# Turning the first step's state back in four events, its split on GpSimd

## The reference, cut to what matters

```python
q = _l2norm(q)
k = _l2norm(k)
state = q
for _ in range(STEPS):          # STEPS = 2, BETA = 1
    sim = jnp.einsum('bqhd,bkhd->bqhk', state, k)
    att = jax.nn.softmax(BETA * sim, axis=-1)
    state = jnp.einsum('bqhk,bkhd->bqhd', att, v)
o = state.reshape(B, S, H) @ Wo + bo
```

## Time and profile before

| what | value |
|---|---|
| median of 3 runs | 3548.38 us (3545.81 to 3549.18) |
| the profiled execution | 3555.46 us |
| its span, first to last instruction | 3553.7 us |
| mean granted TensorE clock | 0.961 |
| PE busy | 3247.1 us, 19974 matmuls |
| DVE busy | 2401.4 us, 5281 instructions |
| ACT busy | 2082.6 us, 2689 instructions |
| POOL busy | 1219.1 us, 2291 instructions |
| costliest group | ACT exponentials (L810), 1574.6 us, 1536 of 1025 ns |
| next | DVE maxima (L1041), 1249.6 us, 1024 of 1220 ns |

### The profile page before, as it was taken

One profiled execution on the slowest core, in us unless ns is written; L12 is line 12 of the kernel. 1 busy time (PEld: TensorE's weight loads), 2 busy tenths in 40 slices (PEclk: granted clock), 3 DMA queues, 4 the chain that ended last, 5 costly groups with the idle time before them and its releaser, 6 DMA issues.

```text
span 3553.7 us, 55360 instructions
## 1 busy us (share of the span) xinstructions
PE 3247.1 (91%) x19974; PEld 1682.0 (47%) x19974; DVE 2401.4 (68%) x5281; ACT 2082.6 (59%) x2689; POOL 1219.1 (34%) x2291
## 2 busy tenths in 40 slices
PE   5888998989999899999999999999999999998999
PEld 2444444444444444454444445444444444444567
DVE  2636675847678676767767676776867677775662
ACT  2454666656666666666666666566666656564442
POOL 3314242342424334242522424252342425222321
PEclk8989999989999999999999999999999999998999
DMA  1000000001110100111001011110001111000110
GB/s 41 4 28 5 31 4 29 31 4 34 31 34 28 31 9 30 34 32 34 29 31 34 5 34 31 34 31 28 34 4 34 31 34 32 30 29 4 59 33 34
DMA packets 81502, 96.89 MB, mean 27 GB/s; under 512 B 50544, under 2 KB 68400, under 8 KB 81104
## 3 DMA queue, kind: packets, MB, share of 16 engines
q1 hardware_dynamic: 81232, 93.35, 8.2%
HBM read 82.76 MB, written 4.78 MB: 25 GB/s over the span
## 4 chain that ended last, share of the span: by engine, by line
PE 53%; DVE 15%; ACT 14%; POOL 10%; issue 7%; SPq 1%; DMA 0%; ACTq 0%; DVEq 0%; POOLq 0%
PE ps L679 14%; PE ps L696 13%; ACT probs L810 12%; PE ps L751 7%; DVE negmax L1041 6%; PE ps L761 5%; PE ps L579 5%; PE ps L716 3%; PE ps L585 2%; PE ps L574 2%; DVE uts L1007 1%; POOL qT L1235 1%; POOL xe L1258 1%; POOL qk L1199 1%; DVE stats L907 1%
## 5 line engine op out<-in xcount | busy, mean ns | idle before, releaser
L810 ACT ACTIVATE probs<-ps 128x1024 f32<-128x1024 f32 x1536 | 1574.6, 1025 | 1070.6 <-PE ps L679 1056.2
L1041 DVE TENSOR_REDUCE negmax<-ps 128x2 f32<-128x1024 f32 x1024 | 1249.6, 1220 | 468.4 <-PE ps L716 451.9
L679 PE MATMUL ps<-qT,kT 32*128 32x512 f32 x3072 | 786.5, 507 | 109.8 <-ACT probs L810 57.4
L696 PE MATMUL ps<-probs,v 128*32 128x512 f32 x6144 | 851.8, 627 | 0.0
L1258 POOL TENSOR_TENSOR xe<-xT_m,G 128x512 f32<-128x512 f32 x288 | 367.2, 1278 | 1045.3 <-PE ps L751 997.2
L751 PE MATMUL ps<-xe,w_sb 128*128 128x256 f32 x2304 | 668.2, 416 | 7.9 <-DVE hid L1100 4.1
L679 PEld LDWEIGHTS ps<-qT,kT 32*128 32x128 f32 x3072 | 291.9, 185 | 763.8 <-ACT probs L810 493.7
L716 PE MATMUL ps<-kT,qT 32*128 32x512 f32 x2048 | 529.4, 512 | 93.7 <-DVE negmax L1041 90.1
L751 PEld LDWEIGHTS ps<-xe,w_sb 128*128 128x128 f32 x2304 | 406.8, 196 | 185.3 <-issue 136.9
L1098 DVE SCALAR_TENSOR_TENSOR th<-th,ps 128x256 f32<-128x256 f32 x576 | 236.8, 411 | 216.6 <-ACT th L840 214.2
L840 ACT ACTIVATE th<-ps 128x256 f32<-128x256 f32 x576 | 221.7, 385 | 180.4 <-PE ps L751 170.1
(11 more groups left out here) (169 smaller groups left out, 2652.8 us busy)
## 6 DMA issues: line engine op xcount, KB each, us to landing
G<-gates_dram SPq DMA_DIRECT2D x96, 768.0 KB, 6.2
maxrow<-negmaxT SPq DMA_DIRECT2D x512, 2.0 KB
v<-v_tok SPq DMA_DIRECT2D x256, 18.0 KB, 1.9
X<-in_x SPq DMA_DIRECT2D x16, 256.0 KB, 2.9
out<-X SPq DMA_DIRECT2D x16, 256.0 KB, 2.3
w_sb<-in_w SPq DMA_DIRECT2D x1, 1152.0 KB, 7.0
w_sb<-in_w SPq DMA_DIRECT2D x1, 576.0 KB, 8.7
gates_dram<-gT SPq DMA_DIRECT2D x32, 18.0 KB
```

The lines of the kernel that those rows point to most:

```text
L679: nc.tensor.matmul(ps[:, B_ST + h, :], kT[a][rows, g * S + kc * P:g * S + (kc + 1) * P], qT[a][rows, g * S:(g + 1) * S], start=True, stop= ...
L696: ins = nc.tensor.matmul(ps[ROWS * j:ROWS * (j + 1), B_UT, :], v[:, at:at + ROWS], probs[:, n % QUADS, j, :], start=(kc == 0), stop=(kc == ...
L810: nc.scalar.activation(probs[:, quad % QUADS, j:j + 2, :], ps[:, B_ST:B_ST + 2, :], ACT.Exp).then_inc(sem["exp_done"], 1)
L1041: nc.vector.tensor_reduce(negative[:, tc, 2 * half:2 * half + 2], ps[:, B_SM:B_SM + 2, :], AX_X, ALU.max, negate=True).then_inc(sem["sm_re ...
```

## The change

VectorE's `uts_state` ends with the first transpose. A new event, `divide`, is placed at w + 11.2: VectorE (lag 0) takes the reciprocal and multiplies there; GpSimd (lag 1.0, so w + 12.2) waits for it and makes both parts of `qstack`. `state` moves from w + 11.2 to w + 13.4: VectorE waits for GpSimd's split and transposes, and GpSimd casts at w + 14.0. Two semaphores, `state_divided` and `state_split`, are added.

```diff
--- before.py
+++ after.py
@@ -47,6 +47,7 @@
 SM_AT = (0, 1, 2, 3, 5, 6, 8, 9)
 JOB = 10
 PV_AT = 3.6
+DIVIDE_AT, STATE_AT = 11.2, 13.4
 S1_AT = (0, 8, 16, 40)
 S2_AT = (48, 64, 80, 88)
 S2_MAX_AT = (31, 42, 63, 73)
@@ -97,7 +98,7 @@
     "dve": {**{n: HOP for n in "sm ffn_y p0_qkv p1_qkv turn o_y m_logits m_down m_probs fold".split()},
             "m_gu": 2.0, "turn": 1.4, "p1_qkv": 1.0, "sm": 0.6, "uts": 0.4, "p0_qkv": 1.0, "ffn_y": 1.0},
     "pool": {**{n: HOP for n in "ffn_stats p0_stats p1_stats m_stats p0_sums p0_hi p1_hi m_index state".split()},
-             "rows": 2 * HOP},
+             "rows": 2 * HOP, "divide": 1.0},
     "sp": {"m_gt": 2 * HOP, "p1_values": HOP},
     "pe": {},
 }
@@ -221,7 +222,8 @@
         t.at(start + 2 * kc + PV_AT, "pv", kind, b, g, kc)
     t.at(start + 10.2, "uts", kind, b, g)
     if kind == "S1":
-        t.at(start + 11.2, "state", b, g)
+        t.at(start + DIVIDE_AT, "divide", b, g)
+        t.at(start + STATE_AT, "state", b, g)
     else:
         t.at(start + 11.2, "turn", kind, b, g)
 
@@ -429,7 +431,7 @@
         gates_in = [ctx.enter_context(nc.semaphore(f"gates_in{i}")) for i in range(3)]
         sem = signals(nc, ctx, "dve_step pool_step "
                                "st_ready exp_done pv_done ut_copied sm_ready sm_read mx_ready "
-                               "state_turned state_done rows_in rows_added o0_part o1_part o_added "
+                               "state_divided state_split state_turned state_done rows_in rows_added o0_part o1_part o_added "
                                "ffn_var ffn_r ffn_biased ffn_done "
                                "p0_var p0_r p0_res p0_squared p0_summed p0_unit p0_hi p0_lo "
                                "p1_var p1_r p1_res p1_hi p1_lo v_moved "
@@ -1006,17 +1008,16 @@
                 dve.wait_ge(sem["pv_done"], TC * (n + 1))
                 nc.vector.transpose(uts[:],
                                     ps[:, B_UT, :]).then_inc(sem["ut_copied"], 1)
-                dve.wait_ge(sem["ut_copied"], n + 1)
+
+            def divide(n, b, g):
+                dve.wait_ge(sem["ut_copied"], window_no("S1", b, g) + 1)
                 link(nc.vector.reciprocal(rden[:], s1t[:, :, HD]))
-                link(nc.vector.tensor_tensor(st8[:], s1t[:, :, 0:HD],
-                                             rden[:].unsqueeze(2).to_broadcast([P, TC * NG, HD]), ALU.mult))
+                nc.vector.tensor_tensor(st8[:], s1t[:, :, 0:HD], rden[:].unsqueeze(2).to_broadcast([P, TC * NG, HD]),
+                                        ALU.mult).then_inc(sem["state_divided"], 1)
 
             def state(n, b, g):
 
-                twice = qstack[:, :, 0:2 * HD].rearrange("p x (r d) -> p x r d", r=2).bitcast(F32R)
-                link(nc.vector.tensor_copy(twice, st8[:].unsqueeze(2).to_broadcast([P, TC * NG, 2, HD])))
-                link(nc.vector.tensor_tensor(qstack[:, :, 2 * HD:3 * HD].bitcast(F32R), st8[:], qstack[:, :, 0:HD],
-                                             ALU.subtract))
+                dve.wait_ge(sem["state_split"], n + 1)
                 nc.vector.transpose(uts[:],
                                     qstack[:].rearrange("p x e -> p (x e)")).then_inc(sem["state_turned"], 1)
 
@@ -1109,7 +1110,7 @@
                                         ALU.add).then_inc(read_signal(key), 1)
 
             play("dve", dict(fold=fold, masks=masks, ffn_stats=ffn_stats, ffn_y=ffn_y, p0_stats=p0_stats, p0_qkv=p0_qkv, p0_sums=p0_sums, p0_hi=p0_hi,
-                      p1_stats=p1_stats, p1_qkv=p1_qkv, p1_hi=p1_hi, turn=turn, uts=uts_state, state=state, sm=sm, mx=mx_turn, o_y=o_y,
+                      p1_stats=p1_stats, p1_qkv=p1_qkv, p1_hi=p1_hi, turn=turn, uts=uts_state, divide=divide, state=state, sm=sm, mx=mx_turn, o_y=o_y,
                       m_stats=m_stats, m_logits=m_logits, m_probs=m_probs, m_index=m_index, m_gu=m_gu, m_down=m_down))
 
         @block.gpsimd
@@ -1224,6 +1225,14 @@
                 pool.wait_ge(sem["p1_hi"], n + 1)
                 low_parts(heads1(i), qk_heads(1, i), i, sem["p1_lo"])
 
+            def divide(n, b, g):
+
+                pool.wait_ge(sem["state_divided"], n + 1)
+                twice = qstack[:, :, 0:2 * HD].rearrange("p x (r d) -> p x r d", r=2).bitcast(F32R)
+                link(nc.gpsimd.tensor_copy(twice, st8[:].unsqueeze(2).to_broadcast([P, TC * NG, 2, HD])))
+                nc.gpsimd.tensor_tensor(qstack[:, :, 2 * HD:3 * HD].bitcast(F32R), st8[:], qstack[:, :, 0:HD],
+                                        ALU.subtract).then_inc(sem["state_split"], 1)
+
             def state(n, b, g):
                 pool.wait_ge(sem["state_turned"], n + 1)
                 nc.gpsimd.tensor_copy(qT[0][:, g * S:(g + 1) * S],
@@ -1259,7 +1268,7 @@
                                         ALU.mult).then_inc(sem["m_xe"], 1)
 
             play("pool", dict(ffn_stats=ffn_stats, ffn_bias=ffn_bias, p0_stats=p0_stats, p0_res=p0_res, p0_squares=p0_squares,
-                      p0_sums=p0_sums, p0_hi=p0_hi, p1_stats=p1_stats, p1_res=p1_res, p1_hi=p1_hi, state=state, rows=rows,
+                      p0_sums=p0_sums, p0_hi=p0_hi, p1_stats=p1_stats, p1_res=p1_res, p1_hi=p1_hi, divide=divide, state=state, rows=rows,
                       m_stats=m_stats, m_index=m_index, m_xe=m_xe))
 
 
```

## The result

The changed kernel takes 3461.8 us in the median of 4 runs (3456.9 to 3464.9) against 3548.8 us for the kernel before: 87 us or 2.5% less, ratio 0.9753 (95% interval 0.9741 to 0.9765). The direction was forecast; the size was not: the forecast was 3498 us, and the range ended at 3465. The profiled execution took 3461.28 us, with a span of 3459.5 us and a mean granted clock of 0.982 (before 0.961).

A forecast was written before the change was run, and what follows sets the result against it. TensorE was taken as the bound, through stalls on VectorE's `negmax`. Stalls of 30 us plus clock of 21 us gave 51 us off, 3497 us for the median, stated as 3498 us, with a range of 3465 to 3542.

The forecast's parts named there:

- The bound: TensorE, busy 91%, bounds the run; its longest waits are for VectorE's `negmax`, 90.1 us in 120 waits.
- The stall term: PE's waits at the four state events shrink by 2.05 us a turn net, 30 us in all.
- The first event: VectorE's transpose alone, without reciprocal and multiply, lets the reduction start earlier: 2.1 us a turn saved.
- The fourth window: Multiply replaces copy, subtract, transpose before a 0.85 us PE wait: 0.7 us saved, at least 0.4 if GpSimd holds it.
- The third event: State's transpose, two slots later ahead of another reduction, costs 0.75 us a turn, 0.5 of it in the first window.
- The clock term: Shorter PE waits spare falls of TensorE's clock: 0.01 in a regular turn's mean clock, 21 us.
- The upper bound of 42 us: Most the clock term could give: 0.02 of clock in each of 14 regular turns.
- GpSimd's part: Copy 0.4 us and subtract 0.45 us, 64 times, 61 us with the link, costed at nothing beside other work.
- The new wait: VectorE's wait for GpSimd's split before the second transpose: margins of 1.5 us or more, costed at nothing.
- Stalls alone: Rival: the waits shrink but the clock falls as before; 30 us gained, 3518 us, chance 0.23.
- taken back: Rival: PE's gain is lost to waits elsewhere in the turn; 0 to 10 us gained, 3543 us, chance 0.10.
- slower by the wait for the split: Rival: VectorE's third event waits for GpSimd, delaying the reduction and PE; 3559 to 3621 us, taken as 3590, chance 0.11.

The follow-up runs named there:

- Experiment 5: Kernel before, with 26 expert half units ahead of the first and second windows' stalled score pairs issued twice: 3509.3 us, ratio 0.9888.
- Experiment 10: Changed kernel with GpSimd's split at 12.0 slots instead of 12.2, ahead of `m_index`: 3460.6 us, ratio 0.9741.
- experiment 9: Changed kernel with the second transpose at 12.4 slots instead of 13.4: 3480.8 us, ratio 0.9806.
- experiment 3: Kernel before with copy, subtract and second transpose at 13.4 slots instead of 11.2, all on VectorE: 3571.3 us, ratio 1.0057.
- Experiment 4: Kernel before with reciprocal and multiply moved from behind the first transpose to the head of the second event at 11.2 slots: 3528.2 us, ratio 0.9926.
- experiment 1: Changed kernel without GpSimd's part: copy and subtract on VectorE, with the second transpose at 13.4 slots: 3517.9 us, ratio 0.9909.

## Why the prediction was right or wrong

*The bound, right.* PE's waits for `negmax` at the four state events were the place; they fell by 37 us where 40 were forecast.

*The stall term, right in its sum.* 2.05 us a turn were forecast. Summed over the regular turns, PE's waits at the state events fell from 4.1 to 1.8 us a turn: 2.26 us, 25 us in 11 turns where 22.6 stood. Experiment 5 gives nearly the same from the times. It has the old stalls and the changed kernel the new ones, at a clock that rounds to 1.00 and 0.99: 2220.9 less 2200.3 is 20.6 us, and to that come 5 to 6 us, since the changed kernel has 17 us more low time. The parts came otherwise than forecast, and two errors cancelled. The first event gave 2.4 us a turn and not 2.1, since PE waits 0.53 and 0.44 us where it had waited 1.30 and 1.20. The fourth window gave 0.33 of 0.85 us and not 0.7. By the text's own figures its lower bound was 1.0 less 0.43, 0.57 us, and not the 0.4 that it names; the measured value lies below both, because the score pair ahead came 0.74 us earlier, and not 0.43, and so took more of that 1.0. The multiply was held by GpSimd, as the row of the held copy had warned and as the Trainium skill (GPSIMD Engine Reference, Specifications) has it for instructions with two SBUF inputs. The trace agrees: 1.02 us beside `xe`, 0.29 without. The third event cost PE a wait of 0.35 us in the first window (0.5 was given) and 0.14 in the second (nothing was).

*The clock term, the step that failed.* "I take the middle, 0.01, 21 us." The price in it was near: 1.5 us per 0.01 of a 205 us turn is 0.37 us for each us of low time, and experiment 5 measured 0.32 to 0.36. The number of falls spared was too small. The regular turns went from 0.97 to 0.99, two times the step taken, and their low time from 137 to 34 us: of their 58.7 us some 25 are stalls and 33 the clock, where 22.6 and 16.5 stood. Over the run the low time went from 277 to 125 us, and 152 us at 0.32 to 0.36 are 49 to 55 us, where 21 stood; that leaves 32 to 38 of the 87 us to the stalls and to what is not accounted for. The trace of the kernel before had the answer. Of the 24 falls in its regular turns, 18 begin between 0.3 us before and 2.4 us behind the end of a wait that the change shortens (10 at the second window's, 4 at the first's, 4 at the fourth's 0.85 us), and these hold 96 of the 137 us; 5 of the others begin at the first window's wait of 0.9 us ahead of its state event, which the change leaves. The prediction had two of the 18 in its rows and named them (the one at 1223.1 begins right at the wait's end, most do not), and still went to the middle between nothing and all, as if nothing were as likely. What is left of the clock's cost fits: of the changed kernel's 8 falls, 5 begin 0.3 to 3.0 us behind that same wait of 0.9 us, three of them around the wait of 0.53 us that now follows it. One of the 5 (timeline, then a stretch, PEclk as the last number but two):

```profile
1370.33 0.50 PE L718 MATMUL ps<-kT,qT 32*128 32x512 f32 x2 [0.90 <-DVE negmax L1042]
```

```profile
1370.80:1374.20 3.40, 3.40 (x13) 1.70 (x16) 3.37 (x7) 0.98 (x2) 2.76 (x8) 0.50 0.02 5
```

The upper bound of 42 us was too low as well, for it left out the irregular parts. What lies outside the 11 turns I had summed at 12 us (three turns more at 3.55 and the 1 us for the first blocks); it gave 35.5 us (22.7 and 12.8), at clocks that went from 0.94 to 0.95 and from 0.95 to 0.98. How much of the start's share is stalls I can't tell; the same kernel again had 10 us less of it.

The Trainium skill (TensorE: Matmul & The Clock Gate, HAM oscillation), which ties falls to longer idle gaps than these and by which the sum would have been 30 us, is not enough for this kernel: experiment 5 took away no stall, only the idleness in two waits of 1.3 and 1.2 us a turn, and the low time fell by 115 us. Nor does the length of a wait alone decide. In the same regular turns PE has 22 waits of 1.0 to 1.3 us at L579, and no fall of the clock begins in the 3 us behind any of them (kernel before, timeline, then a stretch):

```profile
1365.95 0.66 PE L579 MATMUL ps<-id_sb,stack0q 128*128 128x128 f32 x4 [1.33 <-POOL stack0q L1207]
```

```profile
1360.00:1400.00 40.00, 36.32 (x240) 18.95 (x237) 16.71 (x27) 30.13 (x44) 12.05 (x12) 1.00 0.05 8
```

What sets the waits at the state events apart from these was not tried.

*GpSimd's part, right.* 0.40 and 0.46 us, foreseen at 0.4 and 0.45; hidden. *The new wait, right in its cost and wrong in its margin:* 2.9 us in 4 cases, but with 0.03 us to spare in the second window and not 1.5. Experiment 10 shows that VectorE would not have been earlier anyway.

*The signs.* Those of the forecast came: `negmax` waits of 52.8 us, no wait at the third window's first event nor at the fourth's, regular turns at 0.99, hardly any wait for the split. None of them could tell 3498 us from 3462: the low time summed over the run could.

*The rivals.* Stalls alone, taken back, and slower by the wait for the split all fell; experiment 9, which moves the transpose towards the split, still has only 7.4 us of that wait. What I left out was a combination: that the parts would not add up. Alone the later place would have made the kernel slower (experiment 3), with no more waiting for `negmax`, by the clock.

*Open:* why a wait at L579 spares the clock and one as long at a state event does not; the share of stalls in the start's 22.7 us; and why experiment 9 runs its last stretch at a lower clock. Experiment 4 gained 23 us where the profiled execution's waits (8 us less) and low time (9 us less, some 3 us) account for 11. That execution has the lowest clock of its four (0.962; the others 0.965 and 0.966). By the medians of all runs on that chip, 0.9655 against 0.962, the low time is 27 us less, some 9 us, and what stays open is within the interval.

## What to carry to other kernels

When an engine's burst stalls TensorE for about a microsecond, count the stall twice: once as it stands, and once for the clock behind it; here the second was the larger. Look at the granted clock in the stretch right behind each wait of PE, and do so for every fall of the regular turns and not for two: count how many begin at the waits you are removing, and how much low time they hold. Take the price from turns at different clocks, and that share of the sum rather than half of it. A cheap test of such a case is to leave the stall and keep PE busy in it.

## What the runs showed of the hardware

TensorE doing 26 half units twice made the kernel 41 us faster, since the granted clock stayed at 1.00 in turns where it had been 0.97. Waits of PE of 0.85 to 1.4 us at the state events had a fall of the clock beginning at them 18 times in 11 turns, and 22 waits of 1.0 to 1.3 us at L579 not once. The same total of PE's waits (90.5 against 90.1 us), placed otherwise, cost 20 us through the clock (0.951 against 0.961). And a VectorE multiply with two SBUF inputs took 0.8 to 1.0 us beside a GpSimd instruction of 128x512 (`ffn_bias` in the first window, `xe` in the fourth) and 0.29 without one. By moving the division the change put 26 of its 64 cases above 0.5 us where 2 had been (mean 544 ns in place of 315). It is the place that does it, not the split on GpSimd: experiment 1, which has the place alone, has 25 such cases.
